# Softmax, first norm and masks of a fused decoder layer spread anew over the engines

## What is computed

```python
x = x + attn(layernorm(x))        # 16 query heads of 128, one key and value head
x = x + cross(layernorm(x), ctx)  # 16 heads of 32, causal
x = x + ffn(layernorm(x))         # rmsnorm, 32 experts, top 4, and a shared expert

# attn
q = rmsnorm(rope(h @ wq_comp @ wq_up)); k = rmsnorm(rope(h @ wk)); v = h @ wv
scores = where(causal, q @ k.T / sqrt(128), -1e30)
probs = softmax(concatenate([scores, sink]))[..., :t]
out = einsum(probs @ v, out_w1) @ out_w2
# cross
scores = where(causal, qh @ kh.T / sqrt(32), min)
out = (softmax(scores) @ vh) @ Wout.T
```

## Time and profile before

| what | before |
|---|---|
| median of 3 runs | 1214.86 us (1214.48 to 1215.82) |
| profiled execution | 1218.65 us |
| its span | 1216.9 us |
| TensorE busy in the span | 1147.0 us, 94% |
| VectorE | 810.9 us, 67% |
| ScalarE | 596.3 us, 49% |
| GpSimd | 353.8 us, 29% |
| TensorE busy, 300 to 350 us | 49.71 of 50 us |

### The profile page before, as it was taken

One profiled execution on the slowest core, in us unless ns is written; L12 is line 12 of the kernel. 1 busy time (PEld: TensorE's weight loads), 2 busy tenths in 40 slices (PEclk: granted clock), 3 DMA queues, 4 the chain that ended last, 5 costly groups with the idle time before them and its releaser, 6 DMA issues. The chain is left out here.

```text
span 1216.9 us, 20961 instructions
## 1 busy us (share of the span) xinstructions
PE 1147.0 (94%) x7761; PEld 906.3 (74%) x7762; DVE 810.9 (67%) x1392; ACT 596.3 (49%) x1404; POOL 353.8 (29%) x279
## 2 busy tenths in 40 slices
PE   6989999999999999999999999899799999999992
PEld 3457677767776777677777668788599988888892
DVE  1346788789878977897888767532356666666560
ACT  1334565455445645654465435311156666666661
POOL 0011111212221122112211201312236566665753
PEclk9999999999999999999999998999999999999997
DMA  8450000000000000000000023212669999999964
GB/s 276 141 176 9 1 10 9 16 14 9 9 16 14 9 9 15 14 9 9 14 11 6 16 86 128 80 59 68 229 210 269 279 263 266 269 276 264 251 115 59
DMA packets 62597, 121.10 MB, mean 100 GB/s; under 512 B 10128, under 2 KB 13760, under 8 KB 62388
## 3 DMA queue, kind: packets, MB, share of 16 engines
q1 hardware_dynamic: 44820, 82.46, 20.5%
q0 software_dynamic: 17728, 37.97, 14.8%
HBM read 93.55 MB, written 28.13 MB: 100 GB/s over the span
## 5 line engine op out<-in xcount | busy, mean ns | idle before, releaser
L1483 POOL TENSOR_TENSOR rall<-qkv_var,phalf 100x17 f32<-100x17 f32 x16 | 49.2, 3073 | 404.1 <-DVE qkv_var L1163 404.1
L1560 POOL DMA_INDIRECT out_rows<-work,idx x64 | 122.3, 1911 | 120.5 <-issue 86.8
L382 PE MATMUL QS<-xh,wh 128*128 128x256 f32 x512 | 147.8, 289 | 0.0
L383 PE MATMUL QS<-xl,wh 128*128 128x256 f32 x512 | 145.3, 284 | 0.0
L384 PE MATMUL QS<-xh,wl 128*128 128x256 f32 x512 | 145.3, 284 | 0.0
L382 PE MATMUL W<-wch,oth 128*100 128x512 f32 x256 | 105.0, 410 | 0.0
L383 PE MATMUL W<-wcl,oth 128*100 128x512 f32 x256 | 100.7, 393 | 0.0
L384 PE MATMUL W<-wch,otl 128*100 128x512 f32 x256 | 100.4, 392 | 0.0
L383 PEld LDWEIGHTS QS<-xl,wh 128*128 128x128 f32 x512 | 98.7, 193 | 1.2
L382 PEld LDWEIGHTS QS<-xh,wh 128*128 128x128 f32 x512 | 98.6, 193 | 1.2
L384 PEld LDWEIGHTS QS<-xh,wl 128*128 128x128 f32 x512 | 98.5, 192 | 0.0
(11 more groups left out here) (223 smaller groups left out, 2876.5 us busy)
## 6 DMA issues: line engine op xcount, KB each, us to landing
raw<-in_w SPq DMA_DIRECT2D x24, 1024.0 KB, 7.3
raw<-in_w SPq DMA_DIRECT2D x24, 512.0 KB, 9.7
work<-in_w SPq DMA_DIRECT2D x8, 1024.0 KB, 7.1
work<-in_w SPq DMA_DIRECT2D x8, 512.0 KB, 8.7
hx_rows<-h3x SPq DMA_DIRECT2D x16, 212.5 KB
h_columns<-h3s SPq DMA_DIRECT2D x16, 200.0 KB, 1.9
h3T<-h_columns SPq DMA_DIRECT2D x4, 800.0 KB, 9.9
out_rows<-ytiles POOLq DMA_DIRECT2D x16, 200.0 KB, 2.5
```

What stands on the lines that cost most here:

```text
L382: mm(dst, ah, bh, start=start, stop=False)
L383: mm(dst, ah, bl, start=False, stop=False)
L1483: return nc.gpsimd.tensor_tensor(out=dst, in0=src, in1=phalf[:, 0:src.shape[1]], op=ALU.pow)
L1560: nc.gpsimd.indirect_dma_start(out, on_rows(idx[:, NE * j + e:NE * j + e + 1]), Y[e % 2][:, 512 * j:512 * (j + 1)], None, compute_op=ALU.a ...
```

## The change

- *Self softmax.* VectorE takes the maxima of the unscaled scores straight from PSUM, a quarter at a time, and turns them with `rall` and the sink into the negative maxima. ScalarE takes the exponential from PSUM, head by head (16 instructions of 100 columns), with `rall` as scale and the negative maximum as bias. Sums and division run by quarters. The banks are now free at `p_exp`.
- *First norm.* `ln_stats` and `ln1_apply` of batch b+2 run in step b (`R`), behind the routing and ahead of the second norm's apply. The h1 transposes stand behind the first group of self scores.
- *Keys, values, compression* stand ahead of the cross scores, in this order; the *next queries* stand behind the products with the values.
- *Cross mask.* The four mask matmuls are gone. GpSimd masks `PX` in SBUF (`affine_select`, 100x1600), between ScalarE's copy and VectorE's maxima. On VectorE `cross_shifted` moves behind the low parts of the attention outputs.
- On ScalarE the exponentials stand between the copies of h2, cross keys and cross values, the cross scores' copy behind those of the transposed probabilities.

```diff
@@ TensorE
-                for j in range(4):
-                    mm(qb[j][0:T, 0:QW], identb[:, :], mask4[:, :], start=True, stop=False)
...
+                        if i == 0 and do.Q:
+                            ln1_columns(b + 1, wb[0])
                 if do.X:
+                    if do.Q:
+                        pe.wait_ge(s.h1T, b + 2)
                     cross_queries(b, do.C)
...
+                    if do.X:
+                        pe.wait_ge(s.ck, b)
+                    keys_values(b + 1, wb[2])
+                    if do.X:
+                        pe.wait_ge(s.qp, b)
+                    compress(b + 1, wb[1])
                 if do.X:
                     cross_products(b, b + 1, do.C)
...
+                if do.Q:
+                    pe.wait_ge(s.p_exp, 4 * b + 4)
+                    if do.X:
+                        pe.wait_ge(s.sx, 2 * b - 1)
+                    queries(b + 1)
@@ ScalarE
+            def exponentials(i):
+                for h in range(QH * i, QH * (i + 1)):
+                    last = fn(Pm[0:T, T * h:T * (h + 1)], qb[i][0:T, T * (h % QH):T * (h % QH + 1)], ACT.Exp,
+                              bias=mx[:, h:h + 1], scale=rall[:, h:h + 1])
+                last.then_inc(s.p_exp, 1)
@@ VectorE
+                        red(mx[:, QH * i:QH * (i + 1)], qb[i][0:T, 0:QW].rearrange("t (h n) -> t h n", n=T), AX.X, ALU.max)\
+                            .then_inc(s.s_max, 1)
+                    nc.vector.scalar_tensor_tensor(out=mx[:, :], in0=mx[:, :], scalar=-1.0, in1=rall[:, 0:NH], op0=ALU.mult,
+                                                   op1=ALU.mult).then_inc(s.s_shift, 1)
+                    nc.vector.scalar_tensor_tensor(out=mx[:, :], in0=sink[:, :], scalar=-1.0, in1=mx[:, :], op0=ALU.mult,
+                                                   op1=ALU.min).then_inc(s.s_shift, 1)
@@ GpSimd
+            def cross_masked(b):
+                wait_alone(pool, s.sx, 2 * b - 1)
+                nc.gpsimd.affine_select(out=PX[0:T, :].rearrange("t (h n) -> t h n", n=T),
+                                        in_=PX[0:T, :].rearrange("t (h n) -> t h n", n=T), pattern=[[0, NX], [-1, T]],
+                                        compare_op=ALU.is_ge, fill=NEG, base=0, channel_multiplier=1).then_inc(s.sx, 1)
```

More of the change, by code:

```diff
@@ L258, in pipeline @@
             step(1)
-            with eng.Fori(2, NB - 1) as b:
+            with eng.Fori(2, NB - 2) as b:
                 step(b)
+            step(NB - 2)
             step(NB - 1)
@@ L867, in step @@
                     copy(h2T[:, :], wb[0][:, 0:QW]).then_inc(s.h2T, 1)
+                if do.A:
+                    act.wait_ge(s.s_shift, 2 * b + 2)
+                    act.wait_ge(s.pT_ps, 4 * b)
+                    exponentials(0)
+                    exponentials(1)
+                if do.X:
                     act.wait_ge(s.ck_ps, b)
@@ L875, in step @@
                     copy(qpT[:, :], wb[1][:, 0:QW]).then_inc(s.qp, 1)
-                first = isinstance(b, int) and b == 0
-                if first:
-                    joined(range(14, 15))
-                if do.Q and not first:
-                    ln1_columns(b + 1, wb[0])
-                if do.A:
-                    act.wait_ge(s.s_shift, b + 1)
-                    fn(Pm[0:T, :], Pm[0:T, :], ACT.Exp).then_inc(s.p_exp, 1)
-                    act.wait_ge(s.s_sink, b + 1)
-                    act.wait_ge(s.p_den, 2 * b)
-                    fn(esink[:, :], sdiff[:, :], ACT.Exp).then_inc(s.e_sink, 1)
-                if first:
-                    joined(range(15, 16))
-                    ln1_columns(b + 1, wb[0])
+                if isinstance(b, int) and b == 0:
+                    joined(range(14, 16))
+                if do.Q:
+                    compressed(b + 1, wb)
+                    key_square(b + 1)
+                if do.A:
+                    act.wait_ge(s.s_ps, 4 * b + 4)
+                    for i in range(4):
+                        act.wait_ge(s.pT_ps, 4 * b + i + 1)
+                        copy(T16[0:T, QW * i:QW * (i + 1)], wb[i][0:T, 0:QW]).then_inc(s.pT, 1)
                 if do.X:
@@ L1289, in step @@
+                    dve.wait_ge(s.s_shift, 2 * b + 2)
+                    tt(sdiff[:, :], sink[:, :], mx[:, :], ALU.add).then_inc(s.s_sink, 1)
+                if isinstance(b, int) and b == 0:
+                    joined(range(14, 16))
                 if do.C:
@@ L1291, in step @@
                 if do.A:
-                    dve.wait_ge(s.p_exp, b + 1)
-                    red(den[:, :], P3, AX.X, ALU.add).then_inc(s.p_sum, 1)
-                    dve.wait_ge(s.p_sum, b + 1)
+                    for i in range(4):
+                        dve.wait_ge(s.p_exp, 4 * b + i + 1)
+                        red(den[:, QH * i:QH * (i + 1)], P3[:, QH * i:QH * (i + 1), :], AX.X, ALU.add).then_inc(s.p_sum, 1)
+                    dve.wait_ge(s.p_sum, 4 * b + 4)
                     dve.wait_ge(s.e_sink, b + 1)
@@ L1317, in step @@
                     routed(b - 2)
+                if do.R:
+                    if isinstance(b, int) and b < 2:
+                        dve.wait_ge(s.ld_x, 16 * (b + 1))
+                    ln_stats(0, b + 2, s.ln1_stats, s.ln1_var)
                 if do.A:
@@ L1326, in step @@
                     ranked(b - 2)
+                if do.R:
+                    ln1_apply(b + 2)
                 if do.A:
```

131 lines of the change are left out of this document (63 added, 68 removed).

## The result

The changed kernel takes 1220.78 us in the median of 22 runs (1209.81 to 1231.15), the kernel before 1215.36 in 22 runs beside it (1199.28 to 1222.32). The ratio is 1.0066, with a 95% interval of 1.0042 to 1.0089; it goes by the fast runs alone, those within 1.5% of the fastest of their kernel, which leaves out nine of the kernel before and two of the changed one, while the medians of all 22 are only 0.45% apart. The prediction of 3 us more (1218.0, range 1207 to 1232) has the direction right; measured are 5.4 us more.

What follows compares the result with a forecast made beforehand. TensorE bounds the batches, its instructions standing close at 41.40 us a batch. Terms -10.8 + 6.0 + 9.8 - 3.2 + 1.2 = +3.0 us, added to the median 1214.86: about 1218 us, range 1207 to 1232.

Steps and rivals of the forecast that it cites:

- Cross masks off TensorE: Four mask matmuls leave TensorE's queue in batches 1 to 14: 0.77 us a batch, 10.8 us gained.
- First norm ahead of the add: On VectorE its apply delays the residual add x2 by 0.46 us in batches 1 to 13: 6.0 us lost.
- Exponentials at 0.32: ScalarE's 16 exponentials with two tile pointers take 0.32 us each, delaying the cross queries' copy: 9.8 us lost.
- B + 7.96: Cross queries' copy ready 7.96 us after B, the end of a batch's self scores; TensorE wants it at 7.37.
- the 0.59 of the working: TensorE's predicted wait before the compression for ScalarE's copy of the cross queries: 0.59 us a batch.
- the 0.1 that I added for the weight load: Added to TensorE's wait before the compression for the weight load it lays bare: 0.1 us, making 0.7 a batch.
- rival 3: Gains and losses meet: exponentials at 0.29 to 0.31 us, wait about 0.3, 1213 to 1215 us; chance 0.18.
- GpSimd's mask: Masking the cross scores between ScalarE's copy and VectorE's maxima takes 1.8 us and causes no wait in the batches.
- The threshold: Mask duration from which TensorE waits for the cross probabilities: 3.4 us.
- The last batch: Batch 15: transposes 3.1 us earlier, 1.4 from the clock, 1.3 waited for attention outputs; 3.2 us gained.
- if the clock holds: Last batch: without the granted clock's fall to 0.50, the 16 transposes give back another 1.4 us.
- Handover: Toward the shared expert, batch 15's cross maxima start 1.15 us later behind the mask: 1.2 us lost.

Runs made afterwards that it cites:

- e5: Changed kernel with the first norm's statistics and apply moved right behind VectorE's rotated keys, its GpSimd power ahead of the mask: steady batch 41.45 us against 41.92.
- e11: Changed kernel with only GpSimd's four scatters held back until the cross queries are done: steady batch 41.77 us against 41.92.
- e4: Kernel before with only the cross attention's mask moved to GpSimd: steady batch 42.42 us against 41.40.
- e10: Kernel of e8 with ScalarE's copy of h2 between the first and second four exponentials, scatters in place: steady batch 40.61 us.
- e2: Changed kernel with the first norm's apply moved behind the cross attention's residual add, to the end of VectorE's step: steady batch 42.36 us against 41.92.
- e3: Changed kernel with ScalarE's copy of the cross queries ahead of the last four exponentials: steady batch 41.72 us against 41.92.
- e8: Changed kernel with self softmax maxima finished by quarters, exponentials started earlier, first norm as in e5: batch 41.49 us, ratio 1.0033 to the kernel before.
- e7: Changed kernel with GpSimd's mask applied three times over the same scores: steady batch 44.55 us against 41.92.
- e12: Kernel of e10 unchanged, now timed: median 1202.76 us of 6 runs, ratio 0.9862 to the kernel before.
- e9: Kernel of e8 with GpSimd's four scatters of a batch held back until the cross queries are done: steady batch 40.61 us.

## Why the prediction was right, point by point

**Cross masks off TensorE, 0.77 us a batch.** Right, and in full: with the two waits gone the batch is 40.61.

**First norm ahead of the add, 0.46.** Right. The transposes behind it end 0.46 us later than before (the first score mask product stands at 2.10 us after the key transpose, before at 1.64), and e5 takes 0.47 off again.

**Exponentials at 0.32, the copy at B + 7.96, a wait of 0.7.** The 0.32 is exact, the wait is 0.65 with the copy at B + 8.13, and 0.81 a batch from the keys and values to the compression, weight load and all (2.54 against 1.73). The exponentials start 0.2 us late (322.57 is B + 1.44, not 1.24), and this is the late signal for h2's copy in batches 4 to 13, of which nothing could be seen in the trace of before. Where it is on time (batches 1 to 3 and 14, and all of e11) the wait is 0.60 to 0.62: the 0.59 of the working. So the 0.1 that I added for the weight load was not there, and made up for half of the late signal: luck. The steady batch was predicted at 41.8 and is 41.92. Two sums of the prediction are off without bearing on its result: at 0.36 an exponential 16 x 0.04 = 0.64 us more a batch would have been some 9 us dearer, not 7, and rival 3 comes to 1212 at its lower end, not 1213.

**GpSimd's mask, 1.8 us and no cost.** 1.64 us and no cost. The threshold was 0.5 us too high (2.9 against 3.4), and the reason for the cover was incomplete. I counted slack only; e4 shows that GpSimd and VectorE can also hold each other up, and that it matters which of VectorE's operations stands beside the mask.

**The last batch, 3.2 us.** 2.9. Answering to the earlier trace rows, in the changed kernel:

```profile
705.48 1.67 PE L473 MATMUL QS<-ckT,qpT 32*100 32x100 f32 x32 [2.25 <-ACT qpT L815]
707.09 2.39 PE L594 MATMUL W<-ident,work 100*100 100x100 f32 x16
...
713.00 0.56 PE L403 MATMUL W<-ident,h3x 100*128 100x100 f32 x4 [0.81 <-DVE otl L1329]
```

The wait stands before the cross products now and is 2.25 us long instead of 4.66. But the condition "if the clock holds" was not met: the granted clock was at 0.50 here too, from 706 to 708 us (699 to 705 before). The cross products took 1.67 instead of 0.96, so the transposes, at B + 9.67 and not 8.9, came 2.4 us earlier instead of 3.1; they took 2.39 instead of 1.54, so that of the 1.4 some 0.95 came back (from the transposes to those of h3x 5.1 us of work instead of 6.05). The wait for the attention outputs was 0.8, not 1.3. That these misses offset each other is luck.

**Handover, 1.2 us.** 1.3. The cross maxima start 2.0 us after the scaled copy's end instead of 0.8, released by the mask. Answering to the earlier trace rows:

```profile
742.55 1.74 POOL L1532 TENSOR_SCALAR_AFFINE_SELECT work<-work 100x1600 f32<-100x1600 f32 x1 [0.64 <-ACT work L1025]
...
744.33 1.82 DVE L1217 TENSOR_REDUCE mxx<-work 100x16 f32<-100x1600 f32 x1 [1.52 <-POOL work L1532]
```

**What was left out: batches 0 and 1, 2.8 us.** The prediction counts batches 1 to 14 alike, 0.4 us each, and gives batch 0 nothing. Measured are 1.2 us more in batch 0 and 1.7 in batch 1. In batch 0 the keys and values now wait 1.45 us for the low part of the last joined weights (1.07 in the kernel before, where the compression waits, with the transposes of h1 in front). A part that no run here takes by itself, and probably the larger one, is the granted clock. Stretches of the changed kernel behind TensorE's idle time of 2.4 us at the end of batch 0 (the third number from the end is the clock, 1.00 for 2.4 GHz and 0.50 for 1.2):

```profile
107.00:109.00 2.00, 2.00 (x19) 1.96 (x19) 0.77 (x2) 1.81 (x6) 0.26 (x1) 0.76 0.00 0
109.00:111.00 2.00, 2.00 (x14) 2.00 (x13) 0.40 (x1) 0.33 (x1) 0.00 (x0) 0.50 0.03 8
```

In the kernel before the clock stays at 1.00 here, behind an idle time just as long. In e10 it stays so too, but falls behind the 3 us ahead of batch 0 instead:

```profile
68.00:90.00 22.00, 19.54 (x102) 14.39 (x103) 9.45 (x27) 11.49 (x32) 0.00 (x0) 0.85 0.27 86
```

Each of the 13 traces besides that of before shows one of these falls or both, and batches 0 and 1 take 79.5 to 84.9 us in them, where before has 77.4. Whether the kernel before escapes it in most runs, or only in the one that was profiled, these traces do not tell, since there is only one of it. So of these 2.8 us some may be no effect of the change at all.

**Sum.** Predicted +3.0, measured +5.4 (trace +6.1 to the first expert product). The terms that I named (batches 2 to 14, the last batch, the handover) measure 5.7 - 2.9 + 1.3 = 4.1 by the traces, where I had 2.6 (3.0 without the 0.4 of batch 1). The late signal is that difference: with the scatters held back (e11) batches 2 to 14 are 1.5 us shorter. The other 2.0 is batches 0 and 1 (2.8) less 0.8 ahead of and behind them.

## What to carry to other kernels

Where TensorE is the bound and its instructions stand close, moving work off it pays exactly what the instructions took, but only if every result that it wants is ahead of its turn: list for each moved piece both who waits behind it in its queue and who waits for its own result (e2), and start a chain earlier rather than reorder its end (e3 against e8 and e10). Before work goes to GpSimd, look at what VectorE does in that window: an operation with two inputs in SBUF lasted until GpSimd's mask over 1600 columns was done, though not beside its power over 17; so look at both engines' durations in the first trace. And where a stage that a change does not touch differs by 15 us from trace to trace, compare the traces by stages before believing either the two profiled times or a few runs.

## What the runs showed of the hardware that I had not expected

- VectorE's addition of two 100x16 tiles took 1.38 us instead of 0.17 while GpSimd's mask ran, and ended with it (e4, 15 batches). A mask that began during a VectorE operation of that kind took 2.11 us instead of 1.63 (e7, e8, e12, behind the last batch). Beside GpSimd's power (3.07 us, 17 columns) operations of that kind kept their 0.29 us.
- Signals of TensorE were seen late in some arrangements, by ScalarE above all: the copy of h2 0.65 to 0.71 us after the first context product instead of 0.20 (changed kernel, batches 4 to 13), the copy of ck 3.6 instead of 1.1 to 1.6 us after it (e8, batches 4 to 14) and 1.7 to 2.5 instead of 1.09 (e4, batches 4 to 14), while TensorE's products had been done in time. Each of the kernels with the mask on GpSimd and the scatters in their old place shows it, but for e10 and e12; the kernel before does not, and with the mask alone moved (e4) it is there. Holding GpSimd's scatters back ended it both times (e9, e11), another order on ScalarE ended it as well (e10), and neither the kernel before nor batches 3, 14 and 15 of the changed one have it, with their scatters across the same boundary. What exactly it needs is open.
- Of TensorE's idle times of 2.4 and 3 us ahead of batch 1 and of batch 0, now one and now the other was followed by a granted clock down to 0.50, from trace to trace of nearly the same code.
- A mask of 100x1600 in fp32 by GpSimd's affine select took 1.64 us, a little less than VectorE's pass over the same tile (1.82).
